# VectorE's extras inside a selective scan, split into pieces of one or two operations and spread over the scan's steps

## What is computed

```python
emb = tok_table[token_ids] + seg_table[segment_ids] + pos_table[:seq_len][None, :, :]
mu = jnp.mean(emb, axis=-1, keepdims=True)
var = jnp.mean(jnp.square(emb - mu), axis=-1, keepdims=True)
out = (emb - mu) * jax.lax.rsqrt(var + EPS) * gamma + beta
...
h = rmsnorm(x, w_norm1)
z = h @ W_in.T
z = z * jax.nn.sigmoid(h @ W_gate.T)
y = selective_scan(z, W_xproj, W_dt, b_dt, A_log, D_skip)
x = residual + y @ W_out.T
hf = rmsnorm(x, w_ffn_norm)
ffn = jax.nn.silu(hf @ W_gate_ffn.T) * (hf @ W_up.T) @ W_down.T
return x + ffn
```

## Time and profile before

| | |
|---|---|
| median of 3 runs | 1750.38 us (1747.45 to 1765.43) |
| profiled execution | 1742.62 us, span of its instructions 1740.9 us |
| scan stage in it | 96 to 618 us, 522 us for 96 steps |
| busy in the whole span | PE 1355.9 us (78%), DVE 817.2 (47%), ACT 520.3 (30%), POOL 519.9 (30%) |
| granted TensorE clock | 0.866 of full speed |

### The profile page before, as it was taken

One profiled execution on the slowest core, in us unless ns is written; L12 is line 12 of the kernel. 1 busy time (PEld: TensorE's weight loads), 2 busy tenths in 40 slices (PEclk: granted clock), 3 DMA queues, 4 the chain that ended last, 5 costly groups with the idle time before them and its releaser, 6 DMA issues.

```text
span 1740.9 us, 23318 instructions
## 1 busy us (share of the span) xinstructions
PE 1355.9 (78%) x7240; PEld 943.2 (54%) x7240; DVE 817.2 (47%) x1505; ACT 520.3 (30%) x878; POOL 519.9 (30%) x418
## 2 busy tenths in 40 slices
PE   0567678889988874699993778989998889998960
PEld 0223333243254453699883554756657488888850
DVE  2478887777688764011112726355453422222212
ACT  0453444764734410133231313315150101001000
POOL 6366644745654471000003400000001600000025
PEclk9978888888798886899997768898988899999985
DMA  5064433433443313889982100000000388888843
GB/s 126 19 167 113 110 89 85 126 98 85 120 105 85 73 53 111 250 274 274 263 260 73 43 1 1 1 1 0 0 1 10 121 226 239 227 233 236 226 128 95
DMA packets 71614, 206.44 MB, mean 119 GB/s; under 512 B 11360, under 2 KB 32608, under 8 KB 66752
## 3 DMA queue, kind: packets, MB, share of 16 engines
q1 hardware_dynamic: 59648, 181.28, 37.9%
q0 software_dynamic: 11904, 24.40, 4.8%
HBM read 183.42 MB, written 22.22 MB: 118 GB/s over the span
## 4 chain that ended last, share of the span: by engine, by line
PE 35%; DMA 24%; DVE 14%; issue 11%; POOL 6%; POOLq 4%; ACT 2%; DVEq 2%; SPq 1%; ACTq 1%
PE ps L825 22%; DMA expert<-arena 21%; PE ps L956 4%; DVE arena L1498 3%; PE ps L1197 3%; POOL arena L545 2%; PE ps L970 1%; PE ps L986 1%; DMA arena<-sorted 1%; DVE ps L1493 1%; POOLq L536 1%; PE ps L1189 1%; POOL ew_out L454 1%; PE ps L820 1%; ACT arena L787 1%
## 5 line engine op out<-in xcount | busy, mean ns | idle before, releaser
L1498 DVE TENSOR_TENSOR_SCAN arena<-arena,ps 128x1024 f32<-128x1024 f32 x96 | 219.6, 2287 | 25.8 <-ACT arena L686 12.8
L825 PE MATMUL ps<-arena 96*128 96x128 f32 (+1 forms) x1680 | 222.8, 290 | 9.9 <-issue 8.3
L825 PEld LDWEIGHTS ps<-arena 96*128 96x128 f32 (+1 forms) x1680 | 213.6, 191 | 14.7 <-issue 14.5
L825 PE MATMUL ps<-xTF,wreg 96*128 96x512 f32 x352 | 207.1, 736 | 8.8 <-DVE arena L1675 5.0
L533 POOL DMA_DIRECT2D expert<-arena x88 | 47.7, 542 | 493.9 <-DVE arena L1635 270.5
L956 PE MATMUL ps<-arena,pick 32*128 32x512 f32 x384 | 124.6, 739 | 86.9 <-DVE arena L1498 75.3
L412 POOL DMA_INDIRECT sorted<-x_rows,row_i x64 | 63.0, 985 | 409.1 <-DVEq L1414 390.4
L825 PE MATMUL ps<-arena,ew_in 96*128 96x128 f32 x1248 | 150.0, 278 | 8.1 <-issue 7.7
L825 PEld LDWEIGHTS ps<-arena,ew_in 96*128 96x128 f32 x1248 | 145.6, 194 | 11.9 <-issue 11.9
L454 POOL TENSOR_TENSOR ew_out<-arena 128x1024 f32<-128x1024 f32 x48 | 112.6, 2351 | 107.4 <-DVE arena L1498 56.6
L1493 DVE TENSOR_TENSOR ps<-ps,arena 128x1024 f32<-128x1024 f32 x96 | 117.2, 1221 | 58.3 <-PE ps L956 56.3
(11 more groups left out here) (213 smaller groups left out, 1867.8 us busy)
## 6 DMA issues: line engine op xcount, KB each, us to landing
arena<-dt SPq DMA_DIRECT2D x64, 512.0 KB, 4.6
ew_in<-in_e_in SPq DMA_DIRECT2D x24, 768.0 KB, 6.1
arena<-in_e_in SPq DMA_DIRECT2D x24, 768.0 KB, 6.1
ew_in<-dt SPq DMA_DIRECT2D x32, 512.0 KB, 4.8
ew_out<-in_e_out SPq DMA_DIRECT2D x20, 675.0 KB, 6.9
arena<-in_e_out SPq DMA_DIRECT2D x20, 675.0 KB, 7.1
ew_in<-in_e_in SPq DMA_DIRECT2D x20, 576.0 KB, 5.5
arena<-in_e_in SPq DMA_DIRECT2D x20, 576.0 KB, 5.6
```

Of the source, the lines that this page charges most:

```text
L825: last = pe.matmul(o, lhs, rhs, start=(n == 0), stop=(n == len(pairs) - 1))
L1498: ve.tensor_tensor_scan(hid[k % 3], dec[k % 3], bx.rearrange("p x t -> p (x t)"), 0.0, ALU.mult, ALU.add)\
```

## The change

The whole calls on VectorE are taken apart. `stats` does the `bn_stats` of two tiles after a step (`tile_work`); the rest of each norm becomes 13 to 15 "pieces" of one operation each (two in one of them, four `bn_aggr` in another), and `small_work` gives a step five slots for pieces in chunks 0 and 3 and three in chunks 1 and 2. Slot 0 lies between bx and the scan of the step, the others behind the scan. Ahead of each piece stands a drain. The norm of the embedding of chunks 2 and 3, one call before, is done chunk by chunk. The operations of the inverse square root are the same as before; the router's picks and places stay whole and move from steps 10 and 13 to 12 and 15 of chunk 3. The tables of jobs are rewritten to go with it, GpSimd's sums of the embedding are put earlier (chunk 2) and its gathers of chunk 3 later, and the copy of the last two tiles of the feed-forward part (`ldown` 1) goes into the next chunk.

```diff
-        enter_at = {0: [("eturn", 0), ("eturn", 1)], 1: [("egate", 0)], 2: [("egate", 1)], 3: [("egate", 2)], 6: [("ez", 0)],
+        enter_at = {0: [("eturn", 0), ("eturn", 1)], 1: [("egate", 0)], 4: [("egate", 1)], 5: [("egate", 2)], 6: [("ez", 0)],
...
+        leave_late = {0: [("ldown", 1)], 8: [("lnext", 0), ("lnext", 1)], 9: [("lrout", 0)], 10: [("lrout", 1)], 11: [("lscore", 0)]}
...
                     weigh_hidden(c * PAIRS + n)
                     if c == 0:
-                        if n < CT:
-                            embed(3, (n,))
-                        if n == 5:
-                            pool.wait_ge(s_emb[2], 4 * CT * 16)
+                        if n == 0:
+                            pool.wait_ge(s_emb[2], 2 * CT * 16)
                             embed_sum(2)
-                        if n == 6:
+                        if n == 1:
                             embed_pos(2)
+                        if n in (3, 4, 5, 6):
+                            embed(3, (n - 3,))
                         if n == 8:
+                            pool.wait_ge(s_fn, 3)
+                            embed_gamma(2)
+                        if n == 9:
+                            embed_beta(2)
+                        if n == 12:
+                            pool.wait_ge(s_emb[3], 2 * CT * 16)
                             embed_sum(3)
-                        if n == 11:
+                        if n == 13:
                             embed_pos(3)
-                        if n == 14:
-                            pool.wait_ge(s_fn, NCH)
-                            embed_gamma(2)
-                        if n == 15:
-                            embed_beta(2)
-                        if n == 20:
+                    if c == 1:
+                        if n == 0:
+                            pool.wait_ge(s_fn, 4)
                             embed_gamma(3)
-                        if n == 21:
+                        if n == 1:
                             embed_beta(3)
...
-                        if n in (7, 9, 10):
-                            gate_z(c + 1, (7, 9, 10).index(n))
-                        if n == 16:
+                        if n in (7, 8, 10):
...
-                    if c and n in (11, 12):
-                        add_mamba(c - 1, n - 11)
+                    if c and n in (5, 6):
+                        add_mamba(c - 1, n - 5)
...
+            add_scores_bias(NCH - 2)
...
-                    if n == 9 and c:
+                    if n == 0 and c + 1 < NCH:
+                        enter_scale(c + 1)
+                    if c and n == (9 if c == NCH - 1 else 11):
                         leave_scale(c - 1)
...
-                    if n == 14 and c + 1 < NCH:
+                    if n == 15 and c + 1 < NCH:
                         enter_softplus()
...
-            def leave_rms(c):
-                ve.wait_ge(s_mr, 2 * (c + 1))
-                moments(mr, CT)
-                rstd(l_rms[:, :], CT, RMS_EPS, True)
-                ve.drain().then_inc(s_rr, 1)
-
...
+            def stats(src, o, j):
+
+                ve.bn_stats(st[:, o + j, :], src[:, j, :])
+                ve.bn_stats(st[:, o + j + 1, :], src[:, j + 1, :])
+
+            def root_part(i, o, eps, out):
+
+                v, h, y, t = [w[:, o:o + CT] for w in (vv, vh, yy, tt)]
+                if i == 0:
+                    ve.tensor_scalar(v, mv[:, o:o + CT, 1], eps, None, ALU.add)
+                elif i == 1:
+                    ve.tensor_scalar(ti[:, o:o + CT], v.bitcast(I32), 1, None, ALU.logical_shift_right)
+                    ve.tensor_scalar(h, v, -0.5, None, ALU.mult)
+                elif i == 2:
+                    ve.tensor_scalar(y.bitcast(I32), ti[:, o:o + CT], -1.0, float(0x5f3759df), ALU.mult, ALU.add)
+                elif i % 3 == 0:
+                    ve.tensor_tensor(t, y, y, ALU.mult)
+                elif i % 3 == 1:
+                    ve.tensor_tensor(t, t, h, ALU.mult)
+                else:
+                    ve.scalar_tensor_tensor(out=out if i == 11 else y, in0=t, scalar=1.5, in1=y, op0=ALU.add, op1=ALU.mult)
+
+            def gather_part(o):
+                for j in range(CT):
+                    ve.bn_aggr(mv[:, o + j, :], st[:, o + j, :])
+
+            def rms_part(c, i):
+
+                if i == 0:
+                    gather_part(CT)
+                elif i == 1:
+                    ve.tensor_tensor(tt[:, CT:], mv[:, CT:, 0], mv[:, CT:, 0], ALU.mult)
+                elif i == 2:
+                    ve.tensor_tensor(mv[:, CT:, 1], mv[:, CT:, 1], tt[:, CT:], ALU.add)
+                else:
+                    root_part(i - 3, CT, RMS_EPS, l_rms[:, :])
+                if i == 14:
+                    ve.drain().then_inc(s_rr, 1)
...
+            def embed_norm_part(i):
+                if i == 0:
+                    gather_part(0)
+                else:
+                    root_part(i - 1, 0, LN_EPS, n_rstd[:, :])
...
+            def embed_scale(dst, c, j, done=None):
...
+
+            def slots(c):
+                return 3 if c in (1, 2) else 5
+
+            def small_work(c, n, x):
+
+                at = n * slots(c) + x
+                s = slots(c)
+
+                def here(first, parts):
+                    return at - s * first if 0 <= at - s * first < parts else None
+
+                def drained(first, parts):
+                    ve.drain()
+                    return here(first, parts)
+
+                if c == 0:
+                    if here(4, 13) is not None:
+                        embed_norm_part(drained(4, 13))
+                    if here(12, 13) is not None:
+                        embed_norm_part(drained(12, 13))
+                    if here(16, 14) is not None:
+                        embed_rms_part(2, drained(16, 14))
+                    if here(20, 13) is not None:
+                        embed_norm_part(drained(20, 13))
...
+                if c >= 2 and here(3, 14) is not None:
+                    norm_part(c - 2, drained(3, 14))
+                if c and here(6, 15) is not None:
+                    rms_part(c - 1, drained(6, 15))
+                if c == NCH - 1 and here(18, 14) is not None:
+                    norm_part(c - 1, drained(18, 14))
+
+            def tile_work(c, n):
+
+                if c == 0:
+                    h2, h3 = h_rows[:, 2 * CT:3 * CT, :], h_rows[:, 3 * CT:4 * CT, :]
+                    if n == 2:
+                        ve.wait_ge(s_fsum, 3)
+                        stats(h2, 0, 0)
+                    if n == 3:
+                        stats(h2, 0, 2)
...
+                if c:
+                    if n == 4:
+                        ve.wait_ge(s_mr, 2 * c - 1)
+                        stats(mr, CT, 0)
+                    if n == 5:
+                        ve.wait_ge(s_mr, 2 * c)
+                        ve.bn_stats(st[:, CT + 2, :], mr[:, 2, :])
+                        ve.bn_stats(st[:, CT + 3, :], mr[:, 3, :])
...
                 ve.drain()
+                small_work(c, k % PAIRS, 0)
                 ve.wait_ge(s_dec, 2 * k + 2)
...
                 scan_pair(k)
-                if c and n == 7:
-                    leave_rms(c - 1)
-                if c >= 2 and n == 1:
-                    leave_norm(c - 2)
-                if k == 12:
-                    embed_norm(2, 2)
-                if k == 18:
-                    embed_rows(2, 1)
-                if k == PAIRS + 2:
-                    embed_rows(3, 1)
+                for x in range(1, slots(c)):
+                    small_work(c, n, x)
+                tile_work(c, n)
                 if c == NCH - 1:
-                    if n == 10:
+                    if n == 12:
                         ve.wait_ge(s_ch, 2)
                         route_picks(0, E0, 0, 2 * CT)
-                    if n == 13:
+                    if n == 15:
                         bank = seats["rank", c - 1, 1][0]
                         route_places(0, E0, 1, 0, 2 * CT, bank, s_wfree[bank])
-                    if n == 17:
-                        leave_norm(c - 1)
```

More of the change, by code:

```diff
@@ L195, in tower @@
         s_idx, s_sm, s_wa, s_wb = sem("s_idx"), sem("s_sm"), sem("s_wa"), sem("s_wb")
-        s_emb = [sem(f"s_emb{c}") for c in range(3)]
+        s_emb = [sem(f"s_emb{c}") for c in range(4)]
         s_cst, s_neg = sem("s_cst"), sem("s_neg")
@@ L256, in work_at @@
+        rank_at = {14: [("rank", 1)]}
         def work_at(c, n):
-            late = [(what, c - 2, x) for what, x in leave_late.get(n, [])] if c >= 2 else []
+            late = [(what, c - 2, x) for what, x in (late_last if c == NCH - 1 else leave_late).get(n, [])] if c >= 2 else []
             enter = [(what, c + 1, x) for what, x in enter_at.get(n, [])] if c + 1 < NCH else []
@@ L528, in store_blocks @@
+                    if c == NCH - 1 and n in (12, 14):
+                        leave_act(c - 1, n - 12)
+                        leave_act(c - 1, n - 11)
+            add_scores_bias(NCH - 2)
```

(15 more changed lines are left out.)

122 lines of the change are left out of this document (86 added, 36 removed).

## The result

The changed kernel takes 1798.68 us, median of 4 runs (1796.34 to 1809.69); the kernel before, beside it, 1752.64 (1747.45 to 1765.43). The ratio is 1.026, with an interval of 1.0209 to 1.0311: 46 us slower, where +39 and 1789 us were forecast.

A forecast was written before the change was run, and what follows sets the result against it. In the scan, VectorE and TensorE were taken as near their limits, with calls, waits and locks adding time. Terms -15 - 20 + 3 + 96 - 30 + 5 = +39 us gave 1789 us, range 1738 to 1826.

The forecast's parts named there:

- The locks, +96: Scan stage: VectorE's small pieces stand until GpSimd's product ends, 48 steps at 2.0 us, +96 us, ends 43 and 106.
- -20 for those in the calls: Whole calls: time VectorE's small operations lose standing behind GpSimd's elementwise operations goes away, -20 us.
- Waits given back, -30: Scan steps: longer VectorE steps hide waits for TensorE's spread and ScalarE's decay, -30 us, ends 0 and -50.
- Head-of-call waits, -15: Whole calls: VectorE's data waits at the head or inside go, as statistics come several steps after their data, -15 us.
- new waits, +5: Chunk 0, steps 2 and 10: VectorE's statistics wait for GpSimd's queued embedding work, +5 us, range 0 to 11.
- The signs: Changed profile: small operations near 0.8 us, piece steps 6 to 7, GpSimd waiting more for scans, less for TensorE's sums.
- The norm twice, +3.4: Embedding norm: runs twice over four tiles, not once over eight, adding 14 small operations, +3.4 us.
- Jobs moved at no cost: Chunk 3's gathers, the second down-projection job and chunk 2's score bias move without adding time.
- The lock met half as often: Rival, piece steps: TensorE's sums stay late, meetings cost 1.0 us, 48 us in all, total 1741 us; chance 0.20.
- The faster rival: Scan stage: without long calls TensorE's clock stays up, waits fall by 60 us, total 1706 us; chance 0.12.
- break-even: Piece steps: with -30 for waits, the change neither gains nor loses at 57 us of locks, 1.2 per step.
- The last rival: Piece steps: TensorE idles, its clock falls and stays down, +43 us more, total 1832 us; chance 0.08.

The follow-up runs named there:

- e1: Changed kernel with all pieces behind the scan and GpSimd's product of that step released by a drain behind them: 1726.36 us, ratio 0.9875.
- e6: Changed kernel with all pieces behind the scan, GpSimd's product still released by the scan: 1796.58 us, ratio 1.0196.
- e12: Changed kernel with GpSimd's product replaced by a fill with zero, so the result is not fully computed: 1701.6 us, ratio 0.9673.
- e9: Changed kernel with all pieces behind the scan, GpSimd's product alone held behind pieces and scalings, plain steps released by the scan: 1715.07 us, ratio 0.9728.
- e10: Kernel before, norm calls whole, GpSimd's product alone held behind the call in those nine steps, plain steps as they were: 1735.94 us, ratio 0.984.
- e5: Changed kernel with each chain of small operations whole behind one scan, GpSimd's product released behind the chain: 1740.54 us, ratio 0.9908.
- e4: Changed kernel with the down projection's second half back at step 23 of its own chunk: 1803.17 us, ratio 1.0344.
- e7: Kernel before, calls whole, GpSimd's product released by a drain behind the call, or behind the scan in steps without one: 1737.17 us, ratio 0.9928.
- e2: Changed kernel with all pieces of a step between its bx and its scan: 1761.76 us, ratio 1.0084.
- e11: Changed kernel with GpSimd's product replaced by a copy of the scan's result, without the multiplication by C: 1734.35 us, ratio 0.9802.

## Why the prediction was right, step by step

**The locks, +96, and -20 for those in the calls.** Right in kind and place, and near in size. Of the 48 steps counted 42 hold locks behind the scan, 102.5 us or 2.4 each, where 48 x 2.0 = 96 was taken; 2.4 is above the 2.2 of one meeting because some steps hold two, as the one at 304.74 does. By the trace 98 of the 114 us of locks end with the step's product and the rest with other operations of GpSimd. From the rows of the changed kernel the 128x4 pieces last about 101 us longer than alone: L1365 36 x 0.89 = 32, L1367 24 x 0.87 = 21, L1363 36 x 0.435 = 16, L1356 12 x 0.58 = 7, and 25 in ten smaller groups. The sum gave no price of their own to the scalings, two of 128x192 in each of eight steps: 8.8 + 6.6 us for 16 x 0.375 = 6.0, so +9. I had called their number unchanged, which it is; but they too meet the product now. (Four of the 48 steps hold scalings alone, so the +96 has a part of this in it.) The locks of before are 26 us by the same count and not 20: the sum had left out L1286 and the router's 128x8 operations, 2 us each, and smaller ones. Net, the locks grew by 88 us, 12 more than -20 + 96. That it is the locks, e1 against e6 and e12 show. One detail differs: the first piece was to slip in ahead of the product and the second to meet it; at 298.40 the first meets it, 0.01 us late. The price is the same.

**Waits given back, -30.** Measured -28.9. The reason I gave (longer steps hide them) is only a part: in e1 and e9 the steps are short again and the waits are 4.0 and 15.6 us. e9 beside e10 shows 34 us less of them without whole calls, but e5, whole chains with the new tables, has only 17.6 too: what removes them, pieces or tables, is open.

**Head-of-call waits, -15, new waits, +5.** This is the term that failed: 15.4 us became 15.6. The new waits came as forecast, 3.8 + 1.7 for GpSimd's work on the embedding; but of the old ones, taken as gone, 10.1 are left, for ScalarE's queue (7.3, 4.6 before) and for the ranks (2.8, 5.0 before). The largest, 5.4 us at step 0 of chunk 3, is one for the first half of the down projection: the change takes its statistics a step earlier (step 0, not 1) and runs its job a step later (23, not 22), where the sum took the statistics as several steps behind their data and looked only at the second half. With the job back at step 22, in e4, the wait stays at 5.5 us, so what holds it is open. The 10 us of this term and the 12 of the locks are 22; the stage grew by 54 us, 15 more than the 39 forecast, and the 7 between lie in VectorE's short gaps and in operations that overlap in the trace. Part of the closeness is luck: the medians give +46, 7 off, but the two executions whose traces are read here give +54.6, 16 off.

**The signs.** The 128x4 operations have a mean of 0.76 us (0.33 before), as named; steps with pieces last 6.9 us in the mean; GpSimd waits 163 us for scans, 103 before. Two signs are weak: GpSimd's waits for TensorE's sums only fell from 96 to 91 us, so that TensorE catches up in the longer steps is hardly seen, and of the 30 steps that hold nothing but bx and scan half stay under 3.6 us. The forecast's own span, 1765 to 1826, keeps the locks at 96 us; with their ends too, 43 and 106, its terms give 1711 to 1835.

**The norm twice, +3.4.** No run takes it apart. Jobs moved at no cost: e4, and e5 beside e7, agree with that.

**The rivals.** The lock met half as often is refuted, with 114 us of locks. The faster rival is the one that the experiments bear out in part: with most locks gone, the split with its tables is worth some 20 us (e9 against e10), and the granted clock from 100 to 480 us is 0.89 against 0.85, in the mean between the two levels, 1.2 and 2.4 GHz. It needs the locks gone: the changed kernel has no long calls of norms either, and its clock is 0.80. Its break-even was 57 us of locks in the pieces; by the runs, the ratio goes from 0.973 at 17 us (e9) over 1.008 at 78 (e2) to 1.026 at 114, and a line from the first to the second crosses 1 at 64, scalings included. The rule of the Trainium skill (TensorE: Matmul & The Clock Gate, "HAM oscillation — how this bites in real kernels"), cited for this rival, that gaps in TensorE's work throttle its clock, agrees in direction with 0.89 and 0.85. The last rival, the clock falling in the piece steps, is seen in a weak form: 0.80 against 0.82; whether e9's gain is the clock or simply that TensorE gets its next u sooner, no run parts.

## What to carry to other kernels

Before work of one engine is cut into small pieces between the steps of a pipeline, look at what the other engines start at exactly those places: here, in 42 of 48 steps, a piece met an operation of GpSimd, mostly the one of 2.35 us that the same scan had released, and 0.16 us of work became up to 2.4. Count meetings, not work. Once the pieces run first and GpSimd's product is released behind them, the same split pays: 1.026 becomes 0.973. More than half of that gain over the kernel before needs no split: the later release alone brings it to 0.984.

## What the runs showed of the hardware

What stands depends on both operations. Beside GpSimd's elementwise operations that read (a product, 2.35 us, a copy, 1.04) VectorE's small TENSOR_TENSOR, SCALAR_TENSOR_TENSOR and TENSOR_SCALAR that begin under them end with them (67 of 67 in the changed kernel that begin at least 0.2 us before such an operation's end, 62 of 63 in e11); beside a fill, 0.95 us, only TENSOR_SCALAR does. On e12's timeline a TENSOR_SCALAR and a TENSOR_TENSOR with a fill, and between them a TENSOR_TENSOR with a GpSimd operation that reads:

```profile
251.86 0.99 POOL L435 TENSOR_TENSOR h_rows<-h_rows,mr 128x384 f32<-128x384 f32 x1
...
252.68 1.08 DVE L1356 TENSOR_SCALAR ti<-vv 128x4 int32<-128x4 int32 x1
...
252.79 0.95 POOL L455 MEMSET ew_out<- 128x1024 f32 x1
...
255.09 1.27 POOL L426 TENSOR_TENSOR arena<-arena 128x512 f32<-128x512 f32 x1 [1.34 <-ACTq L589]
...
255.28 1.09 DVE L1361 TENSOR_TENSOR tt<-yy 128x4 f32<-128x4 f32 x1
...
258.63 0.95 POOL L455 MEMSET ew_in<- 128x1024 f32 x1 [2.27 <-DVE arena L1661]
258.66 0.16 DVE L1363 TENSOR_TENSOR tt<-tt,vh 128x4 f32<-128x4 f32 x1
```

The scan and bx, which have an operand in PSUM, keep their 2.28 and 1.22 us whatever GpSimd does: over all runs none of them takes longer than 2.29 and 1.23. The Trainium skill (SBUF — State Buffer, "Who interferes with whom") says just this: VectorE and GpSimd have a pair of ports to SBUF in common, taken by one for a whole instruction; VectorE wants it in its two-port modes, which TENSOR_SCALAR can enter, and for a second input from SBUF, the latter only against a GpSimd operation that reads. These numbers agree. It also says that whoever issues first goes first. The TENSOR_SCALAR at 252.68 begins 0.11 us ahead of the fill with which it ends, but GpSimd's operation before that fill (L435, 251.86 to 252.85) is then still running, so it was not first; another of e12, at 202.01, with GpSimd idle and 0.10 us ahead of a fill, goes through in 0.17 us. Three scalings of e12 (128x192, at 137.94, 177.31 and 217.72) do not fit: they begin 0.14 us ahead of a fill, GpSimd idle, and take 1.21 us, to just behind its end. Why is not shown.
